# A state-space block with its state products read from PSUM and its sums accumulated in transposed form

## The reference

```python
def step(state, xs):
    d_t, B_t, C_t, u_t = xs
    dA = jnp.exp(d_t[..., None] * A)
    state = state * dA + (d_t * u_t)[..., None] * B_t[:, None, :]
    y_t = jnp.einsum('ben,bn->be', state, C_t)
    return (state, y_t)
...
y = y + D[None, :, None] * u
y = y * jax.nn.silu(z)
return jnp.swapaxes(y, 1, 2)
...
x = x + _L0_xattn_ref(ctx_1024, _layernorm(x, axis=-1), ...)
x = x + _L0_ffn_ref(_layernorm(x, axis=-1), ...)
```

## Time and profile before

| | us |
|---|---|
| median of 3 runs | 1383.33 (1378.83 to 1387.89) |
| span of the profiled execution | 1381.1 |
| VectorE busy | 868.8 (63%) |
| TensorE busy | 1116.1 (81%) |
| ScalarE busy | 520.5 (38%) |
| GpSimd busy | 606.3 (44%) |

### The profile page before, as it was taken

How to read it: one execution, slowest core, us unless ns; L and a number is a source line. 1 busy time by engine, 2 the same in 40 slices (tenths; PEclk the granted TensorE clock), 3 DMA queues, 4 the chain that set the end, 5 groups by cost and what they waited for, 6 DMA issues and landing times.

```text
span 1381.1 us, 18552 instructions
## 1 busy us (share of the span) xinstructions
PE 1116.1 (81%) x4156; PEld 745.3 (54%) x4156; DVE 868.8 (63%) x745; ACT 520.5 (38%) x697; POOL 606.3 (44%) x424
## 2 busy tenths in 40 slices
PE   4657667677668756763499999999999999999994
PEld 2223222223223322323478888888888888888883
DVE  3799999999999999993732434343253434324321
ACT  3754456555654565222221323232231323213210
POOL 0398498668976798630201222222122222223211
PEclk8688888899778888895599999999999999999998
DMA  5333342336234524334521424242142433414210
GB/s 158 139 122 121 124 137 91 123 121 230 72 110 139 197 91 148 113 104 166 193 107 46 167 101 167 106 164 98 38 160 99 143 124 104 166 48 167 92 40 30
DMA packets 68892, 168.01 MB, mean 122 GB/s; under 512 B 9039, under 2 KB 11599, under 8 KB 68865
## 3 DMA queue, kind: packets, MB, share of 16 engines
q1 hardware_dynamic: 59824, 139.41, 29.4%
q0 software_dynamic: 9040, 28.32, 6.3%
HBM read 343.60 MB, written 18.35 MB: 262 GB/s over the span
## 4 chain that ended last, share of the span: by engine, by line
PE 49%; DVE 2%; DMA 1%; issue 0%; POOL 0%; ACT 0%; POOLq 0%; DVEq 0%
PE hp L1433 10%; PE hp L1432 10%; PE hp L1434 10%; PE yp L1432 5%; PE yp L1434 5%; PE yp L1433 5%; PE tp L1473 2%; PE xp L1426 1%; PE hp L1417 1%; PE yp L1481 0%; DMA work<-xln_dram,index 0%; DMA work<-out_dram,acc_index 0%; DMA out_dram<-work,out_index 0%; DVE R L1299 0%; POOL index L1045 0%
## 5 line engine op out<-in xcount | busy, mean ns | idle before, releaser
L293 POOL TENSOR_TENSOR ring<-du,bc 128x1024 f32<-128x1024 f32 x128 | 361.6, 2848 | 149.2 <-DMA bc<-bcs 80.9
L681 PE MATMUL yacc<-ring,ident 128*128 128x512 f32 x512 | 292.8, 711 | 139.0 <-DVE ring L544 138.2
L532 DVE TENSOR_TENSOR_SCAN ring<-dA,ring 128x1024 f32<-128x1024 f32 x128 | 290.9, 2275 | 6.8 <-ACT dA L356 3.5
L681 PEld LDWEIGHTS yacc<-ring,ident 128*128 128x128 f32 x512 | 106.4, 224 | 308.4 <-DVE ring L544 209.1
L356 ACT ACTIVATE dA<-delta,Acol 128x511 f32<-128x511 f32 (+1 forms) x256 | 165.7, 681 | 223.5 <-DVE ring L532 223.3
L1432 PE MATMUL hp<-w_hi,xT_hi 128*128 128x512 f32 x592 | 237.5, 401 | 0.9 <-DVE xT_lo L1329 0.9
L1433 PE MATMUL hp<-w_lo,xT_hi 128*128 128x512 f32 x592 | 236.6, 400 | 0.0
L1434 PE MATMUL hp<-w_hi,xT_lo 128*128 128x512 f32 x592 | 232.9, 393 | 0.0
L544 DVE TENSOR_TENSOR ring<-ring,bc 128x1024 f32<-128x1024 f32 x128 | 217.9, 1707 | 0.0
L1350 DVE TENSOR_TENSOR work<-hp,work 128x512 f32<-128x512 f32 x74 | 51.0, 690 | 232.3 <-PE hp L1434 194.4
L1069 POOL COPY out_index<-out_tab 128x1 uint32 x37 | 6.7, 181 | 356.4 <-DVE work L1336 356.4
(11 more groups left out here) (177 smaller groups left out, 1186.5 us busy)
## 6 DMA issues: line engine op xcount, KB each, us to landing
stage<-in_L_ffn_w_kernel_dram SPq DMA_DIRECT2D x160, 1024.0 KB
stage<-in_L_ffn_wo_kernel_dram SPq DMA_DIRECT2D x78, 1024.0 KB
bc<-bcs SPq DMA_DIRECT2D x128, 512.0 KB, 4.5
xall<-in_x_dram SPq DMA_DIRECT2D x1, 4096.0 KB, 15.1
xln_dram<-xlnb SPq DMA_DIRECT2D x4, 1024.0 KB, 7.8
out_dram<-xall SPq DMA_DIRECT2D x4, 1024.0 KB, 9.4
ctx_rows<-in_ctx_dram SPq DMA_DIRECT2D x4, 512.0 KB, 4.9
work<-xln_dram,index POOLq DMA_INDIRECT x39, 3.8
```

Of the source, the lines that this page charges most:

```text
L293: g_.tensor_tensor(ring[:, n % RING, :].rearrange("p (e l) -> p e l", e=2), cols(du, b, h * 2 * L, 2 * L).rearrange("p (e l) -> p e l", e= ...
L532: v_.tensor_tensor_scan(ring[:, n % RING, :], dA[n % 2][:, :, :].rearrange("p e l -> p (e l)"), ring[:, n % RING, :], 0.0, ALU.mult, ALU.a ...
L681: last = t_.matmul(yacc[:, e, :], ident[:, :], ring[:, n % RING, e * L:(e + 1) * L], start=False, stop=(n == UPH - 1))
```

## The change

- `times_c` stays on VectorE for all units (`POOL_C` is empty), but reads C from PSUM: TensorE broadcasts one row of C with a matmul (`fill_c`, new line 663) into a single PSUM bank `Cb`. `fill_c(q)` waits until VectorE has finished the product of unit q - 1, and the product of unit q waits for it. Only B still comes through DRAM (`load_B`).
- `dA` becomes three buffers of one bank (half a unit each), and `scan` two instructions of 512 elements (new line 539).
- `acc` becomes eight transposes that accumulate in `yT` (new line 682), so the sum comes out with positions on partitions. The D term becomes eight small matmuls (new line 674). The gate is transposed instead (`zs_T`, 16 transposes a batch and four copies into `zsT`), `y_T` is gone, and `add_y` moves from VectorE (two instructions) to GpSimd (one).
- `silu_z` for the next batch moves next to `silu_u`, behind unit 18. Other tasks move by a few units.
- All four batches are written out; there is no loop.

`ffn_block` is the same.

```diff
+SB = 3
+LEAD = 4
+LAG = 2
...
+POOL_C = ()
...
+        bB = sb("bB", [P, 4, 2, L])
+        bC = sb("bC", [P, 4, L])
...
-        dA = [ctx.enter_context(nc.psum_tensor(f"dA{i}", [P, 2, L], fp32)) for i in range(2)]
-        yacc = ctx.enter_context(nc.psum_tensor("yacc", [P, 2, L], fp32))
+        dA = [ctx.enter_context(nc.psum_tensor(f"dA{i}", [P, L], fp32)) for i in range(SB)]
+        Cb = ctx.enter_context(nc.psum_tensor("Cb", [P, L], fp32))
+        yT = ctx.enter_context(nc.psum_tensor("yT", [P, LB, 2 * P], fp32))
...
+            def add_y(b, h):
+                pool.wait_ge(y_gated, 2 * b + h + 1)
+                xs = xall[:, b * LB:(b + 1) * LB, h * 2 * P:(h + 1) * 2 * P]
+                g_.tensor_tensor(xs, g[:, :, :], xs, ALU.add).then_inc(x_added, 1)
...
+                    if s == 8 and b > 0:
+                        add_y(b - 1, 1)
...
+            def exp_dA(q):
+                b, h, n = UNIT[q]
                 if n == 0:
-
...
-                    last = a_.activation(dA[n % 2][:, e, 1:L], cols(delta, b, eb * L + 1, L - 1), ACT.Exp,
-                                         scale=Acol[:, eb, n:n + 1])
...
+                    r, eb = 2 * q + e, 2 * h + e
+                    if r >= SB:
+                        act.wait_ge(scan_done, r - SB + 1)
+                    a_.activation(dA[r % SB][:, :], db(b, eb * L, L), ACT.Exp, scale=Acol[:, eb, n:n + 1]).then_inc(exp_done, 1)
...
+                    if s == 3 and not rest:
+                        guess_1()
...
+                    if s == 6 and not rest:
+                        silu_z(b)
...
+                    if s == 18 and nxt:
+                        silu_u(b + 1)
+                        silu_z(b + 1)
+                    if s == 19 and rest:
+                        gate_T(b - 1, 0)
+                        gate_T(b - 1, 1)
...
-            def scan(b, h, n):
-
-                dve.wait_ge(exp_done, q0(b, h) + n + 1)
-                dve.wait_ge(dbu_done, q0(b, h) + n + 1)
-                v_.tensor_tensor_scan(ring[:, n % RING, :], dA[n % 2][:, :, :].rearrange("p e l -> p (e l)"), ring[:, n % RING, :],
-                                      0.0, ALU.mult, ALU.add).then_inc(scan_done, 1)
-
-            def times_c(b, h, n):
...
-                C = bc[:, c % 4, 1, n % 2:n % 2 + 1, :].to_broadcast([P, 2, L])
-                states = ring[:, n % RING, :].rearrange("p (e l) -> p e l", e=2)
-                v_.tensor_tensor(states, states, C, ALU.mult).then_inc(hc_done, 1)
...
+            def scan(q):
+                dve.wait_ge(dbu_done, q + 1)
+                for e in range(2):
+                    r = 2 * q + e
+                    dve.wait_ge(exp_done, r + 1)
+                    o = ring[:, q % RING, e * L:(e + 1) * L]
+                    v_.tensor_tensor_scan(o, dA[r % SB][:, :], o, 0.0, ALU.mult, ALU.add).then_inc(scan_done, 1)
+
+            def times_c(q):
+                dve.wait_ge(scan_done, 2 * q + 2)
+                dve.wait_ge(C_full, NTH_DVE[q] + 1)
+                states = ring[:, q % RING, :].rearrange("p (e l) -> p e l", e=2)
+                v_.tensor_tensor(states, Cb[:, :].unsqueeze(1).to_broadcast([P, 2, L]), states, ALU.mult).then_inc(hc_dve, 1)
...
+                    scan(q)
+                    if q - 1 in NTH_DVE:
+                        times_c(q - 1)
+                    if s == 2 and rest:
+                        drain_y(b - 1, 1)
...
+                    if s == 7 and rest:
+                        stats_2(b - 1)
+                    if s == 8 and nxt and not rest:
+                        conv(b + 1, (0, 1))
+                    if s == 11 and nxt and rest:
+                        conv(b + 1, (0, 1))
+                    if s == 15 and nxt:
+                        conv(b + 1, (2, 3))
...
+                if rest and nxt:
+                    logit_copy(b - 1)
+            if NU - 1 in NTH_DVE:
+                times_c(NU - 1)
+            logit_copy(NB - 2)
...
+            def fill_c(q):
+
+                b, h, n = UNIT[q]
+                k = USE[f"XP.{b}"]
+                if n < 2:
+                    pe.wait_ge(freed[k % 2], nth(k))
+                if NTH_DVE[q] > 0:
+                    pe.wait_ge(hc_dve, NTH_DVE[q])
+                at, rows = DR + DS + n, DR + 2 * DS
+                t_.matmul(Cb[:, :], ident[0:rows, at:at + 1].to_broadcast([rows, P]), xdbl[:, b % 2, :], start=True, stop=True).then_inc(C_full, 1)
...
+                    for t in range(LB):
+                        for e in range(2):
+                            t_.matmul(yT[:, t, e * P:(e + 1) * P], ub(b, (2 * h + e) * L + t * P, P), diagD[:, 2 * h + e, :],
+                                      start=(t % 2 == 0 and e == 0), stop=False, skip_group_check=True)
...
-                        t_.matmul(yacc[:, e, :], diagD[:, 2 * h + e, :], cols(u, b, (2 * h + e) * L, L), start=True, stop=False)
...
-                    last = t_.matmul(yacc[:, e, :], ident[:, :], ring[:, n % RING, e * L:(e + 1) * L], start=False, stop=(n == UPH - 1))
+                        last = t_.matmul(yT[:, t, e * P:(e + 1) * P], ring[:, q % RING, e * L + t * P:e * L + (t + 1) * P], ident[:, :],
+                                         start=False, stop=(n == UPH - 1), is_transpose=True, skip_group_check=True)
                 last.then_inc(acc_done, 1)
...
+                    if q in NTH_DVE:
+                        fill_c(q)
+                    if q >= LAG:
+                        acc(q - LAG)
...
+                    if s == 8 and nxt and rest:
+                        in_proj(b + 1, (0, 1))
...
+                    if s == 12 and nxt:
+                        in_proj(b + 1, (2, 3))
...
+                    if s == 19 and nxt:
+                        x_proj(b + 1)
...
+                    if s == 31 and rest:
+                        logits_of(b - 1)
+            for q in range(NU - LAG, NU):
+                acc(q)
```

More of the change, by code:

```diff
@@ new lines, in q0, with ub, db, dub @@
+        def q0(b, h):
+            return b * UPB + h * UPH
+        def ub(b, lo, n):
+            return u[:, b % 2, lo:lo + n]
+        def db(b, lo, n):
+            return delta[:, b % 2, lo:lo + n]
+        def dub(b, lo, n):
+            return du[:, b % 2, lo:lo + n]
+        def row(t, b, i):
+            return t[:, b * LB + i, :]
+        def units():
+            for b in range(NB):
+                for h in range(2):
+                    for n in range(UPH):
+                        yield q0(b, h) + n, b, h, n
@@ L185, in _ @@
+        UNIT = {q: (b, h, n) for q, b, h, n in units()}
+        NU = len(UNIT)
+        ON_POOL = [q for q in UNIT if UNIT[q][2] in POOL_C]
+        ON_DVE = [q for q in UNIT if UNIT[q][2] not in POOL_C]
+        NTH_POOL = {q: j for j, q in enumerate(ON_POOL)}
+        NTH_DVE = {q: j for j, q in enumerate(ON_DVE)}
+        block = ctx.enter_context(nc.Block())
         @block.sync
@@ new lines, in ctx_T, with in_proj @@
+                    last.then_inc(done, 1)
+            def in_proj(b, ebs):
+                for i in range(KB):
+                    k = USE[f"T{i}.{b}"]
+                    pe.wait_ge(freed[k % 2], nth(k))
+                for eb in ebs:
+                    o, done = use(f"X{eb}.{b}")
+                    for i in range(KB):
+                        last = t_.matmul(o[:, :], wT[:, i, eb * P:(eb + 1) * P], ctxT[:, i, :], start=(i == 0), stop=(i == KB - 1))
+                    last.then_inc(done, 1)
@@ L736, in gate_T, with zs_T @@
+            def zs_T(b, ts):
+                pe.wait_ge(zs_ready, b + 1)
+                for t in ts:
+                    o, done = use(f"Z{t}.{b}")
+                    for i in range(LB):
+                        last = t_.transpose(o[:, i * P:(i + 1) * P], zs[:, i * L + t * P:i * L + (t + 1) * P], ident[:, :])
+                    last.then_inc(done, 1)
+            def gate_T(b, i):
                 pe.wait_ge(xln_done, b * LB + i + 1)
-                k = uses["G%d" % i]
-                use(k, turn)
+                o, done = use(f"G{i}.{b}")
@@ L801, in _ @@
+            o, done = use("DTT")
             for eb in range(EB):
-                last = t_.transpose(bank(k)[0:DR, eb * P:(eb + 1) * P], dt_rows[:, eb, :], ident[:, :])
-            last.then_inc(filled[k % 2], 1)
-            ctx_T(0, FIRST, 0)
-            for eb in range(EB):
-                in_proj(FIRST, 0, eb)
-            x_proj(0, FIRST, 0)
-            for eb in range(EB):
-                dt_proj(FIRST, 0, eb)
-            turn(0, TURN0, 0, rest=False)
-            with pe.Fori(1, NB - 1) as b:
-                turn(b, LOOP, b - 1)
```

822 lines of the change are left out of this document (403 added, 419 removed).

## The result

Before and after, three runs each: 1383.33 us (1378.83 to 1387.89) and **1413.38 us** (1411.04 to 1415.04); ratio 1.0227, 95% interval 1.0183 to 1.0271. The change made the kernel slower by 30 us, where 1365 was forecast; the range reached to 1405. The profiled execution took 1409.3 us.

The account below looks back on a forecast made before the run. VectorE was taken to bound the stretch from 56.9 to 617.4 us. Work -64.1, old waits -4.6, new waits +47.4 and the end +2.8 gave -18.5 on 1381.1, 1362.6; with 2.2 for the runs' median 1365 us, range 1335 to 1405.

Parts of the forecast that it names:

- waits behind `in_proj`, `x_proj`, nine: Batches 0 to 2: eight-instruction TensorE tasks overrun the slot and delay the fill of C, nine times 2.4, 21.6 us.
- logits in the stage, two: Batches 1 and 2: VectorE's logit copy right behind product 30 waits 5.4 us for TensorE, twice, 10.8 us.
- ScalarE (`dA`): VectorE waits for exponentials behind long SiLU work with fewer `dA` buffers: 6.9 us, plus 2.8 in batch 0.
- end, last product to statistics: After the last product, logits, last sums, drain and GpSimd's `add_y` take 8.8 us instead of 6.0, +2.8.
- only by company: VectorE's product: slow only beside GpSimd's, both reading SBUF; from PSUM 1.210 for 1.707 us, 128 times, -63.6 us.
- TensorE's clock: In the unit stage, transposes count like matmuls and a nearly always busy TensorE returns from 1.2 to 2.4 GHz.
- slot rule at 1.2 GHz: TensorE between products: a 4.5 us slot holds fill and transposes, 1.8 us, or 3.5 at 1.2 GHz.
- almost none: Room for another TensorE task in a 4.5 us slot at 1.2 GHz, against up to 2.7 us at 2.4.
- rival 1: Every `fill_c` slot: TensorE stays at 1.2 GHz; 1423 us, or some 1480 if throughout; waits over 66 us; chance 0.17.
- Rival 3: VectorE's product gets no faster, as `ring` in SBUF still lets GpSimd hold it up; 1.707 stays, 1429 us; chance 0.03.
- Rival 2: VectorE's waits are hidden: TensorE at 2.4 GHz for long tasks, ScalarE less late; 1332 us; chance 0.17.
- Rival 4: More in-order waits than counted (copies to banks, B rows at a batch's start), none long; 1375 to 1395 us; chance 0.08.

Follow-up runs that it names:

- experiment 2: Against the kernel after the change, the fill of C contracts over 128 rows (48 to 127 zero) instead of 48; 1361.3 us.
- experiment 6: Against the kernel after the change, C rows come by DMA and the product reads both inputs from SBUF, transposes stay; 1360.8 us.
- experiment 4: Against the kernel after the change, zero-weight matmuls or zero-tile transposes added in 18 task-free slots a batch; 1386.1 us with matmuls, 1385.3 with transposes.
- experiment 1: Against the kernel after the change, logits in four parts, copies three units later, context and gate transposes behind, last sums first at the end; 1406.4 us.
- the one execution of 1519.8 us: One of four executions of the kernel with the fill over 128 rows, at mean clock 0.72, left out of its ratio; 1519.8 us.

## Why the prediction was wrong

The terms, in us, with what the kernel after showed and what the kernel of experiment 2 did, which differs from it by the zero rows and by setting them to zero at the start:

| term | predicted | after (48 rows) | 128 rows |
|---|---|---|---|
| product | 1.210 | 1.214 | 1.204 |
| scan half | 1.208 | 1.204 | 1.205 |
| VectorE's work in the stage | 492 | 491.4 | 488.5 |
| waits behind `in_proj`, `x_proj`, nine | 21.6 | 26.3 | 20.7 |
| waits behind `dt_proj`(second), three | 0 | 10.6 | 1.8 |
| 0.43 in each plain slot | 0 | 12.5 | 0 |
| logits in the stage, two | 10.8 | 19.4 | 11.1 |
| ScalarE (`dA`) | 9.7 | 3.9 | 8.0 |
| end, last product to statistics | 8.8 | 14.4 | 10.2 |
| clock in the stage | "2.4 GHz for most" | 0.68 | 0.88 |
| time | 1365 | 1413.4 | 1361.3 |

*Right:* what bounds the kernel, the price of the product from PSUM and of the scan halves, `add_y` off VectorE at no cost, and where the new waits would stand (fill behind long tasks, logits, the end). With TensorE at 2.4 GHz their sizes too: in the column for 128 rows each wait is within two microseconds of the predicted one and VectorE's work 3.5 below it (waits in its stage 45.4 us, 47.4 predicted). That the product was slow "only by company" holds in kind (experiment 6 gives the spread back), though its size there does not: 30 us of the 63 are PSUM's.

*The step that failed* is the last one under "TensorE's clock": "transposes raised the clock like matmuls, and a TensorE that falls to 1.2 GHz, where it is nearly always busy (3.5 of 3.4 us), comes back". Its first half held (experiment 4). Its second half took every busy microsecond to be alike. The stretches on which it rested were full of products and transposes over 128 rows; the new unit is for half of its time a fill over 48, and in this kernel TensorE then stays at 1.2 GHz for up to 44 us while it is busy without a gap. What it cost: waits of 90.3 us in the stage where 47.4 were counted, and 1413.4 us against 1361.3 with 128 rows. It was also given 1.2 GHz in places where the prediction saw none, out of full work (304.7 us). Over 128 rows the clock holds through all of 517 to 595 us, most of it plain slots in which TensorE is idle for a third of the time.

*A second, smaller error* is in the slot rule at 1.2 GHz. It counted 3.5 us and let a slot of 4.5 hold it. The fill takes 2.01 and the sums 1.89 there, 3.90 in all; and the 4.5 was worked out from a fill at 2.4 GHz. At 1.2 GHz nothing is left for any task, and a unit is 0.43 us longer than VectorE's work even without one. So "almost none" was in truth less than none, and the second `dt_proj` of a batch, priced at nothing, costs 3.54 a time.

*The rivals.* What happened is rival 1, TensorE at 1.2 GHz: its mark, over 66 us of waits with the clock near 0.5 in long stretches, is met (90.3 in the stage). It had 0.17. Its two prices, 1423 and 1480, lie on the far side of 1413, since TensorE had 2.4 GHz for a third of the stage (mean 0.68). What it named as the cause, a TensorE that stands still behind each convolution, is not the main one: the kernel with 128 rows has the same convolutions and a clock of 0.88. Rival 3 is out (1.214, hardly any spread). Rival 2 was never near: even with the clock kept up, waits were 45 us. Rival 4's waits exist but are small; ScalarE's fell to 3.9 in the kernel after and were 8.0 with 128 rows; that a VectorE which waits for TensorE gives ScalarE time is the likely reason, not a tested one (the 14.1 of experiment 1 have their own, given there).

What stays open: from how many rows the clock holds, whether `dt_proj` with its 16 rows matters too (it was never widened), which part of the change gave the other 33 us of the product, and what the one execution of 1519.8 us was.

## What to carry to other kernels

When a change gives TensorE small products (a broadcast by a one-hot column, a low-rank projection), look at how many rows they contract over, and read the granted clock beside the busy time: busy and at 0.50 meant here that the work did not hold the clock, and zero rows up to 128 made no product longer and won 52 us. A buffer in PSUM with one bank, refilled by an engine that works in order, turns every other task of that engine into a wait; cut such tasks to the room that a slot leaves, at the slower clock as well. When a wait is taken away, look for it at the next engine: here moving the logits gave 7 us for 17 us of waits taken away.

## What was not expected of the hardware

With the fill over 48 or 64 rows the mean clock was 0.69 and 0.68, over 96 or 128 rows 0.86 and 0.88, with the same durations at either clock (48 rows 589 to 1219 ns, 128 rows 592 to 1222): 1413 and 1400 against 1365 and 1361 us. The Trainium skill (TensorE: Matmul & The Clock Gate, Part 2) says that the number of rows does not matter for the time that loading the weights takes; this trace agrees (the fill's weight loads took 182 to 335 ns over 48 rows and 185 to 338 over 128). The product's own time did not depend on it either, as the rows of experiment 2 show; for the clock it mattered most. TensorE can thus be busy for 25.00 of 25.00 us at 1.2 GHz, and adding work that computes nothing (experiment 4) made the whole kernel 27 us faster. And VectorE's and GpSimd's products, both from SBUF, slow each other down (1.451 and 3.036 us on average); with C in PSUM they are 1.214 and 2.352.
